# Row maxima of causal attention: narrow products that share a PSUM bank, and another order of the units

## The chip, the cores and the metric

The kernel runs on one core of a Trainium2 chip. The metric is the device time of one execution in microseconds (us). TensorE (PE in the profile, PEld for its weight loads) does the matrix products, VectorE (DVE), ScalarE (ACT) and GpSimd (POOL) work beside it, and SyncE (SP) issues the transfers. PSUM is the memory that TensorE writes: eight banks, each of 512 f32 columns on 128 partitions.

## What is computed

The input x is 4 sequences of 1024 tokens with 128 channels. First comes a causal attention with 16 heads of 8 channels, on a layer norm of x:

```
Q, K, V = heads of (x @ W_dq) @ W_uq, (x @ W_dkv) @ W_uk, (x @ W_dkv) @ W_uv
scores  = Q K^T / sqrt(8), keys after the query masked
out     = softmax(scores) V @ W_o
x       = x + layernorm(out)
```

Then two layers of windowed attention with a gated MLP follow, on a layer norm of x. The change touches only the causal attention, and in it only the maxima of the rows of the scores, which the softmax subtracts before the exponential.

## The kernel before, in words

**Stages and groups.** The causal attention works through 16 stages. A stage is one sequence and four heads (HG = 4). For each stage the scores are computed twice. The first time queries lie on the partitions, so that VectorE can take each query's maximum over the keys. The second time keys lie on the partitions, with the negated maximum added inside the product (12 further rows of the operands), so that ScalarE can take exp at once and TensorE can multiply by V. The second pass of a stage is 12 groups (EXP_GROUPS, L316), n0 to n11 below: n0 to n3 belong to the first 512 queries, with 512, 384, 256 and 128 columns, n4 to n11 to the other 512, with 512 columns in n4 to n8, then 384, 256 and 128. Each group has four score products, one for each head.

**The units of the maxima.** The first pass is cut into units (MAX_UNITS, L315): row tile i (128 queries, 0 to 7), head j, block kc of 512 keys. Row tiles 0 to 3 need one block (128, 256, 384, 512 columns), row tiles 4 to 7 a whole block of 512 and a second one of 128, 256, 384 or 512 columns. That makes 48 units a stage. The last block of a row tile crosses the diagonal: VectorE adds the mask and takes the maximum in one custom instruction, followed by a read of the accumulator (L1491). The whole block before it takes a plain reduction (L1493). The order before is row tile, head, block, so from row tile 4 on a wide whole block and a narrow masked one alternate.

**How the two passes are woven.** Units run ahead of the groups: 32 before the first group, then 8 a group for the first six groups of the kernel, then 4 a group (max_until, L324). So in every stage from the second on, units of the coming stages are spread like this: n0 has row tile 2, n1 row tile 3, n2 and n3 row tile 4, n4 and n5 row tile 5, n6 and n7 row tile 6, n8 and n9 row tile 7, n10 row tile 0, n11 row tile 1. In TensorE's program (L1011) each of a group's four score products is followed by a quarter of the group's units. After the units come, where they are due, the turning of the maxima (turn_maxima, L728) and of the outputs (turn_outputs, L738), and after every odd group the products with V of two earlier groups (values, L712). "The pair n2/n3" below is two groups with their V products. V products that begin a new half of the queries also wait for ScalarE's copy of the finished output (copy_outputs, L1104).

**The ring.** Unit products go to the tensor psM, four banks used in turn (MRING = 4, m_bank). Every unit has a slot of its own (max_slot, L355). The turned outputs of the attention take slots of the same ring (o_slot, L361). TensorE waits with a unit until VectorE has read the slot four before it:

```
ge(pe, m_read, r - MRING + 1)
```

VectorE waits with slot r until `m_ready` is r + 1 and adds one to `m_read` with each unit (maximum, L1482). merge (L1495) joins the two blocks' maxima after the last unit of a stage, outputs (L1500) divides the turned outputs, and GpSimd's cut_maxima (L1329) splits the maxima into three bf16 parts. They are turned, copied by ScalarE and sent by SyncE to the operand (send_maxima, L621), and the second pass of the stage needs them. The scores of the second pass have a ring of three banks (psE), in which narrow groups already share a bank (score, L696).

**Work of other parts in this stretch.** In stages 4 to 6, 8 to 10 and 12 to 14 the output projection and two layer norms of the sequence before are also done, with VectorE's statistics (moments_m, L1522) between the maxima.

Of the kernel before, what the change touches and what calls it, by code (L numbers as in the profile page):

```python
# [21 lines left out]
ALU = mybir.AluOpType  # L22
ACT = mybir.ActivationFunctionType
AX = mybir.AxisListType

B, S, D = 4, 1024, 128
P = 128
NT = B * S // P
TB = S // P
NCH = NT // 4  # L30
NH, DK, DC = 16, 8, 32
HG = 4
# [3 lines left out]
ROWS = NPAIR * DK  # L36
# [5 lines left out]
NEG = -1e30  # L42
# [10 lines left out]
def ge(eng, sem, count):  # L53

    if isinstance(count, int) and count <= 0:
        return
    eng.wait_ge(sem, count)
# [254 lines left out]
            pipelined(pe, NCH, 2, [(2, transposes), (3, heads)])  # L312


MAX_UNITS = [(i, j, kc) for i in range(TB) for j in range(HG) for kc in range(i // 4 + 1)]  # L315
EXP_GROUPS = [(qc, kt) for qc in range(2) for kt in range(4 * qc + 4)]  # L316
NMU, NGR = len(MAX_UNITS), len(EXP_GROUPS)
NM_A = sum(1 for i, _, _ in MAX_UNITS if i < 4)
NSTAGE = B * NG
# [3 lines left out]

def max_until(G):  # L324

    return max(0, min(NSTAGE * NMU, LEAD + min(FAST * (G + 1), SKEW + HG * (G + 1))))


def max_group(u):

    G = -1
    while max_until(G) <= u:
        G += 1
    return G


def o_turn_group(e, qc):

    return e * NGR + (8 if qc == 0 else NGR + 4)
# [12 lines left out]
    return (4, 4, 2, 1)[max(0, kt - 4 * qc)]  # L352


def max_slot(u):  # L355

    G = max_group(u)
    return u + sum(1 for e in range(NSTAGE) for qc in range(2) if o_turn_group(e, qc) < G)


def o_slot(e, qc):  # L361

    G = o_turn_group(e, qc)
    return max_until(G) + sum(1 for e2 in range(NSTAGE) for q2 in range(2) if o_turn_group(e2, q2) < G)


def masks_until(G):
# [36 lines left out]


E_SLOT, E_TOTAL = e_slots()
M_TAIL = NSTAGE * NMU + 2 * NSTAGE - 3
LAST_G = NSTAGE * NGR - 1


def m_bank(r):

    return r % 4 if r < M_TAIL else 2


def in_output_bank(b, h, project):

    return b == B - 1 and (h == 1 or project)
# [70 lines left out]
def attend_and_layers(nc, io, sb):  # L489


    with ExitStack() as ctx:
        def early(name, shape, dt=F32):
            return ctx.enter_context(nc.sbuf_tensor(name, shape, dt))

        def sem(name):
            return ctx.enter_context(nc.semaphore(name))

        arena = sb["arena"]
        NPROB, NRING, MRING = 5, 3, 4  # L500
        qs, ks, v_flat = sb["qs"], sb["ks"], sb["v_flat"]
# [4 lines left out]
        nm = early("a_nm", [P, 2, 2, TB, HG])  # L506
# [59 lines left out]
        with ExitStack() as banks:  # L566
            psM = banks.enter_context(nc.psum_tensor("a_psM", [P, MRING, 512], F32))
# [14 lines left out]
        m_ready, m_read = sem("m_ready"), sem("m_read")  # L582
# [100 lines left out]
        def _(pe):  # L683
            def max_unit(u):

                s, (i, j, kc) = u // NMU, MAX_UNITS[u % NMU]
                g, r = s % NG, max_slot(u)
                if u % NMU == 0:
                    pe.wait_ge(stack_in[g], 32 * (s // NG + 1))
                n = min(512, (i + 1) * P - 512 * kc)  # L690
                out = psM[:, m_bank(r), 0:n]
                ge(pe, m_read, r - MRING + 1)
                pe.matmul(out, qs[0:ROWS, g, j, i * P:(i + 1) * P], ks[0:ROWS, g, j, 512 * kc:512 * kc + n],  # L693
                          start=True, stop=True).then_inc(m_ready, 1)

            def score(G, j):  # L696

# [40 lines left out]
            def turn_outputs(e, qc):  # L738
                r = o_slot(e, qc)
                pe.wait_ge(o_copied, 2 * e + qc + 1)  # L740
                if r < M_TAIL:
                    ge(pe, m_read, r - MRING + 1)
                elif r < M_TAIL + 2:
                    pe.wait_ge(m_read, r)
                    pe.wait_ge(hT_copied, r - M_TAIL + 2)
                out = psM[:, m_bank(r), :] if r < M_TAIL + 2 else psO
                for t in range(4):
                    mm = pe.transpose(out[:, t * P:(t + 1) * P], oT[:, qc, t * P:(t + 1) * P], sb["ident"])
                mm.then_inc(m_ready, 1)
# [14 lines left out]
            def project_o(b, h):  # L764
# [6 lines left out]
                if in_output_bank(b, h, True):  # L771
                    pe.wait_ge(m_read, M_TAIL + 3)
                    out, done = psO, m_o_done
# [234 lines left out]
            for u in range(max_until(-1)):  # L1008
                max_unit(u)
# [468 lines left out]
        def _(dve):  # L1478
# [3 lines left out]
            def maximum(u):  # L1482
                s, (i, j, kc) = u // NMU, MAX_UNITS[u % NMU]
                r = max_slot(u)
                n = min(512, (i + 1) * P - 512 * kc)
                if s > 1 and u % NMU in (0, NM_A):
                    dve.wait_ge(nm_parts, 2 * (s - 2) + (u % NMU == NM_A) + 1)
                dve.wait_ge(m_ready, r + 1)
                scores, low = psM[:, m_bank(r), 0:n], nm[:, s % 2, kc, i, j:j + 1]
                if kc == i // 4:  # L1490
                    dve.tensor_tensor_reduce(scores, scores, sb["mask_q"][:, 512 - n:512], -1.0, -3.0 * NEG, ALU.add, ALU.min, low).then_inc(m_read, 1)  # L1491
                else:
                    dve.tensor_reduce(low, scores, AX.X, ALU.max, negate=True).then_inc(m_read, 1)  # L1493

            def merge(s):  # L1495
                dve.wait_ge(m_read, max_slot(s * NMU + NMU - 1) + 1)
# [485 lines left out]
```

## Time and profile before

| | us |
|---|---|
| three runs: median (lowest, highest) | 1361.78 (1360.88, 1364.80) |
| profiled execution, its own time | 1359.25 |
| profiled execution, span from first to last instruction | 1357.5 |
| causal attention's groups, first to last score product | about 83 to 583 |
| mean granted TensorE clock over the span | 0.97 of full |

The table's first line is what the forecast is compared with. The profile is one execution, and durations come from it. In the profile a line number is that of the kernel before. A matmul's recorded duration holds its way through the array, so two matmuls overlap in the record; the distance between two starts tells what one costs the engine. The rows themselves stand in a section of their own below.

### The profile page before, as it was taken

The page shows a single profiled execution, that of the slowest core. Times are in us where ns is not written, and L with a number is a line of the kernel's source. Part 1 is how long each engine was busy: PE and PEld are TensorE (multiplying, and loading weights), DVE is VectorE, ACT ScalarE, POOL GpSimd, SP SyncE. Part 2 cuts the span into 40 slices and gives each one's busy share as a digit, 9 for nine tenths or more (in the row PEclk, how much of TensorE's full clock was granted, in tenths as well). Part 3 has the DMA queues.
Part 4 walks back from the last instruction along what each step waited for, and adds up shares of the span by engine and source line. Part 5 has one row for each costly group of instructions (what it writes and reads, how often), then busy time and mean ns, then how long its engine had stood idle before and what let it go on. Part 6 is the DMA issues. An engine that isn't in the chain of part 4 may idle for free. (4 is left out here: it accounts for less than half of the span.)

```text
span 1357.5 us, 30203 instructions
## 1 busy us (share of the span) xinstructions
PE 1235.0 (91%) x10501; PEld 702.8 (52%) x10501; DVE 1116.1 (82%) x2928; ACT 926.9 (68%) x2463; POOL 745.5 (55%) x753
## 2 busy tenths in 40 slices
PE   4689999999999999888899999799899999997895
PEld 2323434434433443356666666566466666666663
DVE  5788888988898889679799999766589999997675
ACT  4526776777787777577888888533588888885344
POOL 1112211332231133378999999533699999997244
PEclk9959999999999999899999999899999999999998
DMA  4432111111111101011111111100112111111001
GB/s 109 131 101 75 45 56 46 58 55 52 51 39 42 55 21 35 25 33 36 42 33 33 29 29 33 48 0 1 24 25 54 33 33 33 25 33 25 1 17 47
DMA packets 35486, 56.46 MB, mean 42 GB/s; under 512 B 6898, under 2 KB 22652, under 8 KB 33020
## 3 DMA queue, kind: packets, MB, share of 16 engines
q1 hardware_dynamic: 34760, 54.39, 15.3%
q8 instruction: 85, 1.39, 0.4%
q14 instruction: 65, 0.53, 0.1%
q10 hardware_dynamic: 576, 0.15, 0.1%
HBM read 27.78 MB, written 8.39 MB: 27 GB/s over the span
## 5 line engine op out<-in xcount | busy, mean ns | idle before, releaser
L1095 ACT ACTIVATE a_prob<-a_psE 128x512 f32<-128x512 f32 (+1 forms) x608 | 306.3, 582 | 137.6 <-PE a_psE L707 136.2
L693 PE MATMUL a_psM<-a_ks,a_qs 72*128 72x512 bf16 (+3 forms) x768 | 249.1, 344 | 12.8 <-DVE a_nm L1493 5.2
L1491 DVE CUSTOM_DVE_ANT_0 a_psM<-a_psM,mask_q 128x384 f32<-128x384 f32 (+3 forms) x512 | 242.0, 507 | 13.7 <-PE a_psM L693 13.2
L1327 POOL TENSOR_SCALAR_AFFINE_SELECT a_prob<-a_prob 128x512 f32<-128x512 f32 x128 | 81.3, 638 | 312.3 <-ACT a_prob L1095 311.2
L707 PE MATMUL a_psE<-a_qs,a_ks 84*128 84x512 bf16 (+3 forms) x768 | 240.4, 334 | 11.5 <-ACT a_prob L1095 5.9
L1386 POOL TENSOR_TENSOR w_rn<-w_ssm,mhalf 128x16 f32<-128x16 f32 x64 | 220.3, 3443 | 48.8 <-DVE w_ssm L1581 33.4
L1493 DVE TENSOR_REDUCE a_nm<-a_psM 128x1 f32<-128x512 f32 x256 | 175.4, 685 | 45.3 <-PE a_psM L693 45.3
L1205 ACT ACTIVATE w_prob<-w_psS,w_bias 128x128 f32<-128x128 f32 x512 | 179.9, 377 | 21.0 <-DVE w_bias L1607 20.9
L1371 POOL TENSOR_TENSOR w_t<-w_raw,w_sin 128x256 f32<-128x256 f32 x252 | 176.4, 733 | 0.0
L1376 POOL TENSOR_TENSOR w_rot<-w_t,w_t 128x1024 f32<-128x1024 f32 x63 | 148.5, 2357 | 8.6 <-issue 0.4
L707 PEld LDWEIGHTS a_psE<-a_qs,a_ks 84*128 84x128 bf16 x768 | 74.8, 99 | 149.2 <-ACT a_prob L1095 66.1
L723 PE MATMUL psO<-a_prob,v_all 128*32 128x512 f32 (+3 forms) x1536 | 148.2, 502 | 0.0
L806 PE MATMUL w_psQK<-w_wqkv,w_hT 128*128 128x512 f32 x256 | 120.9, 593 | 1.4 <-DVE w_t L1588 1.4
L693 PEld LDWEIGHTS a_psM<-a_ks,a_qs 72*128 72x128 bf16 x768 | 76.1, 99 | 84.3 <-DVE a_nm L1491 27.2
L1205 ACT ACTIVATION_READ_ACCUMULATOR w_prob<-w_psS,w_bias 128x1 f32 x512 | 111.1, 217 | 0.0
L1607 DVE TENSOR_REDUCE w_bias<-w_psS 128x4 f32<-128x512 f32 x128 | 87.7, 686 | 25.9 <-PE w_psS L851 25.6
L828 PE MATMUL w_psT_<-ident,w_rot 128*128 128x128 f32 x512 | 70.6, 282 | 33.7 <-DVE w_rot L1596 26.8
L828 PEld LDWEIGHTS w_psT_<-ident,w_rot 128*128 128x128 f32 x512 | 56.4, 143 | 79.8 <-DVE w_rot L1596 68.5
L1596 DVE TENSOR_TENSOR w_rot<-w_rot,w_rn 128x1024 f32<-128x1024 f32 x64 | 77.9, 1218 | 23.5 <-POOL w_rot L1376 23.5
L1212 ACT ACTIVATE w_pT<-w_psT_ 128x512 f32<-128x512 f32 x64 | 38.2, 597 | 71.2 <-PE w_psT_ L860 71.2
L860 PE MATMUL w_psT_<-ident,w_prob 128*128 128x128 f32 x512 | 80.6, 281 | 2.9 <-DVE w_prob L1620 2.5
L1620 DVE TENSOR_TENSOR w_prob<-w_prob,w_rden 128x1024 f32<-128x1024 f32 x64 | 78.5, 1227 | 2.2
(189 smaller groups left out, 2386.8 us busy)
## 6 DMA issues: line engine op xcount, KB each, us to landing
a_qs<-q_parts SPq DMA_DIRECT2D x16, 576.0 KB
a_ks<-k_parts SPq DMA_DIRECT2D x16, 576.0 KB
q_parts<-p_parts SPq DMA_DIRECT2D x24, 128.0 KB
k_parts<-p_parts SPq DMA_DIRECT2D x24, 128.0 KB
w_vb__707<-w_v__691 SPq DMA_DIRECT2D x16, 128.0 KB, 2.2
w_vb__708<-w_v__691 SPq DMA_DIRECT2D x16, 128.0 KB, 2.3
w_vb__708<-w_v__692 SPq DMA_DIRECT2D x16, 128.0 KB, 2.2
w_vb__709<-w_v__692 SPq DMA_DIRECT2D x16, 128.0 KB, 2.4
```

The costliest lines, as they stand in the source:

```text
L693: pe.matmul(out, qs[0:ROWS, g, j, i * P:(i + 1) * P], ks[0:ROWS, g, j, 512 * kc:512 * kc + n], start=True, stop=True).then_inc(m_ready, 1)
L707: mm = pe.matmul(psE[:, r % NRING, j % share * w:(j % share + 1) * w], ks[0:KROWS, g, j, kt * P:(kt + 1) * P], qs[0:KROWS, g, j, q0:q0 + w ...
L723: mm = pe.matmul(psO[32 * j:32 * j + 32, q0:512], v_flat[:, col + j * VA:col + j * VA + 32], prob[G % NPROB][:, j, 0:512 - q0], start=(kt ...
L806: pe.matmul(psQK[:, w, :], hT[T % 2][:, 0:P], wqkv[:, first:first + INNER], start=True, stop=True).then_inc(qk_done, 1)
L828: i = pe.transpose(psT[w][:, c * P:(c + 1) * P], rot[:, T % 2, w * INNER + c * P:w * INNER + (c + 1) * P], sb["ident"])
L1095: act.activation(prob[G % NPROB][:, j - share + 1:j + 1, 0:w], psE[:, r % NRING, 0:share * w].rearrange("p (j n) -> p j n", j=share), ACT. ...
L1205: i = act.activation(w_prob[:, p, w, c, :], psS[:, w, c * P:(c + 1) * P], ACT.Exp, bias=bias[:, p, n:n + 1], accum_out=den[:, p, n:n + 1])
L1371: i = pool.tensor_tensor(out[:, w, :, half, :], src[:, w, :, 1 - half, :], tab, ALU.mult)
L1376: pool.tensor_tensor(rot[:, T % 2, :], t1[:, T % 2, :], t2[:, :], ALU.add).then_inc(rot_done, 1)
L1386: pool.tensor_tensor(rn[:, T % 2, 0:n], ssm[:, T % 2, 0:n], sb["mhalf"][:, 0:n], ALU.pow).then_inc(rn_done, 1)
L1491: dve.tensor_tensor_reduce(scores, scores, sb["mask_q"][:, 512 - n:512], -1.0, -3.0 * NEG, ALU.add, ALU.min, low).then_inc(m_read, 1)
L1493: dve.tensor_reduce(low, scores, AX.X, ALU.max, negate=True).then_inc(m_read, 1)
```

## The change

The order of the units becomes row tile, block, head. A function max_width gives a unit's columns, max_share how many consecutive units use one bank: four units of 128 columns, two of 256, one of 384 or 512. m_slots hands out the slots in the order of TensorE's program, units of one bank with one slot together, so a stage takes 38 slots for its units where it took 48. TensorE waits for a free bank only before the first unit of a bank and signals only after the last; VectorE waits before the first and signals after the last.

```diff
-MAX_UNITS = [(i, j, kc) for i in range(TB) for j in range(HG) for kc in range(i // 4 + 1)]
+MAX_UNITS = [(i, j, kc) for i in range(TB) for kc in range(i // 4 + 1) for j in range(HG)]
...
+def max_width(u):
+
+    i, _, kc = MAX_UNITS[u % NMU]
+    return min(512, (i + 1) * P - 512 * kc)
+
+
+def max_share(u):
+
+    return max(1, 512 // max_width(u) if max_width(u) != 384 else 1)
+
+
+def m_slots():
+
+    slots, n = {}, 0
+    for G in range(-1, NSTAGE * NGR + HG):
+        for u in range(max_until(G - 1) if G >= 0 else 0, max_until(G)):
+            slots["u", u] = n
+            if u % max_share(u) == max_share(u) - 1:
+                n += 1
+        for e in range(max(0, G // NGR - 1), min(G // NGR + 1, NSTAGE)):
+            for qc in range(2):
+                if o_turn_group(e, qc) == G:
+                    slots["o", e, qc] = n
+                    n += 1
+    slots["o", NSTAGE - 1, 1] = n
+    return slots, n + 1
...
-M_TAIL = NSTAGE * NMU + 2 * NSTAGE - 3
+M_TAIL = M_TOTAL - 3
...
                 n = min(512, (i + 1) * P - 512 * kc)
-                out = psM[:, m_bank(r), 0:n]
-                ge(pe, m_read, r - MRING + 1)
-                pe.matmul(out, qs[0:ROWS, g, j, i * P:(i + 1) * P], ks[0:ROWS, g, j, 512 * kc:512 * kc + n],
-                          start=True, stop=True).then_inc(m_ready, 1)
+                share = max_share(u)
+                at = u % share * n
+                if u % share == 0:
+                    ge(pe, m_read, r - MRING + 1)
+                mm = pe.matmul(psM[:, m_bank(r), at:at + n], qs[0:ROWS, g, j, i * P:(i + 1) * P], ks[0:ROWS, g, j, 512 * kc:512 * kc + n],
+                               start=True, stop=True)
+                if u % share == share - 1:
+                    mm.then_inc(m_ready, 1)
...
-                dve.wait_ge(m_ready, r + 1)
-                scores, low = psM[:, m_bank(r), 0:n], nm[:, s % 2, kc, i, j:j + 1]
+                share = max_share(u)
+                at = u % share * n
+                if u % share == 0:
+                    dve.wait_ge(m_ready, r + 1)
+                scores, low = psM[:, m_bank(r), at:at + n], nm[:, s % 2, kc, i, j:j + 1]
                 if kc == i // 4:
-                    dve.tensor_tensor_reduce(scores, scores, sb["mask_q"][:, 512 - n:512], -1.0, -3.0 * NEG, ALU.add, ALU.min, low).then_inc(m_read, 1)
+                    d = dve.tensor_tensor_reduce(scores, scores, sb["mask_q"][:, 512 - n:512], -1.0, -3.0 * NEG, ALU.add, ALU.min, low)
                 else:
-                    dve.tensor_reduce(low, scores, AX.X, ALU.max, negate=True).then_inc(m_read, 1)
+                    d = dve.tensor_reduce(low, scores, AX.X, ALU.max, negate=True)
+                if u % share == share - 1:
+                    d.then_inc(m_read, 1)
```

max_slot and o_slot now look the slot up in that table. No instruction on data is added or taken away on any engine.

## Rows read from the trace of the kernel before

**Rows 1.** The page's head: busy time, share of the span, instructions of each engine.

```profile
PE 1235.0 (91%) x10501; PEld 702.8 (52%) x10501; DVE 1116.1 (82%) x2928; ACT 926.9 (68%) x2463; POOL 745.5 (55%) x753
```

**Rows 2.** Busy time by stretch: length, PE, PEld, DVE, ACT, POOL, clock, DMA share, GB/s.

```profile
103.29:111.39 8.10, 7.74 (x45) 3.11 (x45) 7.15 (x24) 5.15 (x9) 0.00 (x0) 0.86 0.59 151
...
156.10:185.00 28.90, 28.13 (x212) 11.36 (x208) 25.15 (x85) 20.60 (x42) 6.71 (x16) 1.00 0.18 52
...
246.26:275.61 29.35, 28.48 (x213) 11.54 (x209) 27.56 (x102) 23.39 (x50) 10.72 (x19) 1.00 0.19 58
275.61:305.07 29.46, 28.41 (x213) 11.20 (x209) 26.25 (x93) 23.40 (x50) 8.54 (x18) 1.00 0.20 58
```

**Rows 3.** Waits in stage 2 (156.1 to 185): total us, times, longest.

```profile
DVE a_nm L1493 <- PE a_psM L693: 2.6, 3, 1.5
...
DVE a_psM L1491 <- PE a_psM L693: 1.0, 1, 1.0
```

**Rows 4.** Waits of stages 1 to 14 (127.09 to 543.6), TensorE for VectorE.

```profile
PEld a_psM L693 <- DVE a_nm L1491: 14.4, 51, 0.5
...
PEld a_psM L693 <- DVE a_nm L1493: 12.2, 31, 0.5
...
PEld a_psM L693 <- DVE o_tok L1509: 4.5, 14, 0.3
```

**Rows 5.** Timeline of PE, pair n2/n3 of stage 2: start us, duration us, instruction.

```profile
160.80 0.28 PE L707 MATMUL a_psE<-a_qs,a_ks 84*128 84x256 bf16 x1
160.91 0.38 PE L693 MATMUL a_psM<-a_ks,a_qs 72*128 72x512 bf16 x1
161.13 0.27 PE L707 MATMUL a_psE<-a_qs,a_ks 84*128 84x256 bf16 x1
...
162.15 0.39 PE L693 MATMUL a_psM<-a_ks,a_qs 72*128 72x512 bf16 x1
...
162.96 0.39 PE L693 MATMUL a_psM<-a_ks,a_qs 72*128 72x512 bf16 x1 [0.24 <-DVE a_nm L1493]
...
163.24 0.22 PE L693 MATMUL a_psM<-a_ks,a_qs 72*128 72x128 bf16 x1
163.39 1.71 PE L723 MATMUL psO<-a_prob,v_all 128*32 128x512 f32 x16
```

**Rows 6.** Timeline of DVE, the same pair.

```profile
161.40 0.69 DVE L1493 TENSOR_REDUCE a_nm<-a_psM 128x1 f32<-128x512 f32 x1
162.01 0.29 DVE L1491 CUSTOM_DVE_ANT_0 a_psM<-a_psM,mask_q 128x128 f32<-128x128 f32 x1
...
162.22 0.69 DVE L1493 TENSOR_REDUCE a_nm<-a_psM 128x1 f32<-128x512 f32 x1
...
165.68 0.69 DVE L1493 TENSOR_REDUCE a_nm<-a_psM 128x1 f32<-128x512 f32 x1 [0.90 <-PE a_psM L693]
```

**Rows 7.** Timeline of ACT, the same pair: the copy of the finished output.

```profile
162.00 0.59 ACT L1108 ACTIVATE a_oT<-psO 128x512 f32<-128x512 f32 x1
```

**Rows 8.** Timeline of PE, pair n10/n11 of stage 2.

```profile
182.13 0.22 PE L693 MATMUL a_psM<-a_ks,a_qs 72*128 72x128 bf16 x1
182.19 0.22 PE L707 MATMUL a_psE<-a_qs,a_ks 84*128 84x128 bf16 x1
...
183.15 0.28 PE L693 MATMUL a_psM<-a_ks,a_qs 72*128 72x256 bf16 x1
183.36 1.71 PE L723 MATMUL psO<-a_prob,v_all 128*32 128x512 f32 x16
```

**Rows 9.** Timeline of DVE, the same pair.

```profile
181.99 0.30 DVE L1491 CUSTOM_DVE_ANT_0 a_psM<-a_psM,mask_q 128x128 f32<-128x128 f32 x1
...
182.20 0.33 DVE L1491 CUSTOM_DVE_ANT_0 a_psM<-a_psM,mask_q 128x128 f32<-128x128 f32 x1
...
182.45 0.33 DVE L1491 CUSTOM_DVE_ANT_0 a_psM<-a_psM,mask_q 128x128 f32<-128x128 f32 x1
```

**Rows 10.** Timeline of PE at the kernel's first group.

```profile
83.43 0.61 PE L707 MATMUL a_psE<-a_qs,a_ks 84*128 84x512 bf16 x1 [4.09 <-DMA a_qs<-a_nmT]
```

More of the change, by code:

```diff
@@ L352, in exp_slots @@
     return (4, 4, 2, 1)[max(0, kt - 4 * qc)]
+def max_width(u):
[17 more added lines that the diff above has]
+    return slots, n + 1
+M_SLOT, M_TOTAL = m_slots()
 def max_slot(u):
-    G = max_group(u)
-    return u + sum(1 for e in range(NSTAGE) for qc in range(2) if o_turn_group(e, qc) < G)
+    return M_SLOT["u", u]
 def o_slot(e, qc):
-    G = o_turn_group(e, qc)
-    return max_until(G) + sum(1 for e2 in range(NSTAGE) for q2 in range(2) if o_turn_group(e2, q2) < G)
+    return M_SLOT["o", e, qc]
 def masks_until(G):
```

## The prediction

> **What bounds the kernel now.** I read the page's head first [rows 1]: TensorE is busy for 91% of the span and VectorE for 82%, too close together to name a bound. The change lies in the causal attention alone, so I cut that into its stages. A plain stage takes 28.90 us, with VectorE busy for 25.15 and ScalarE for 20.60 [rows 2]. TensorE shows 28.13, but its records overlap. No engine is full in such a stage: the period comes from engines that wait for each other by turns. VectorE waits 2.6 + 1.0 us a stage for unit products [rows 3], mostly once a pair, while TensorE does the products with V and has at most four units handed over. TensorE in turn waits for VectorE to free a bank [rows 4]: 14.4 + 12.2 + 4.5 = 31.1 us over stages 1 to 14, or 2.2 a stage. Those rows are of the weight loads and overcount, since the product in front is often still running. So the question is what each of these waits holds up, and that shows only in the order of time, pair by pair.
>
> In **pair n2/n3** (row tile 4) [rows 5], cost goes by columns: from 160.80 to 160.91 a score product of 256 columns takes 0.11, from 160.91 to 161.13 a unit of 512 takes 0.22. So 128 columns cost about 0.06. The unit at 162.15 waits for the reduction that started at 161.40 and ended 0.69 later, at 162.09 [rows 6]; the one at 162.96 waits again, for the reduction of 162.22 to 162.91. By columns the whole pair would have been issued 0.7 us sooner than it was. In **pair n10/n11** (row tiles 0 and 1) the units of 128 columns run freely up to 182.13, but the last of 256 columns is issued at 183.15 [rows 8]. A score product of 128 and a unit of 256 cost 0.17 together; they come 0.25 apart instead, because each unit waits for a 128-column read and VectorE does those every 0.25 us [rows 9]. In n8/n9 one unit waits 0.3 for outputs() (14 times in 14 stages, the third row of [rows 4]); in n4/n5 and n6/n7 of a plain stage no unit waits.
>
> **The change, part by part.** All counts of instructions stay, on every engine and queue. What changes is the order, and where the waits stand.
>
> *Pair n2/n3.* Now four units of 512 columns come first, into four banks, and then four of 128 into one bank. By columns: 160.80 + 4 x 0.33 = 162.12 for the start of n3's first score product, 162.18 for its first narrow unit. That unit needs the bank of the first wide one, whose read ends at 162.09 as before, so it hardly waits. The other three don't wait at all. Four times 0.11 leads to a last unit at about 162.5 and, 0.15 later as in [rows 5], the V products at 162.65. They also wait for ScalarE's copy of the output, 162.00 + 0.59 = 162.59 [rows 7]; that is just in time and is what is late next. V products start at 163.39 now. **Gain 0.74.**
>
> *Pair n10/n11.* Four units of 128 columns share a bank, and the 256s use two. The last 256 is issued at 182.19 + 0.06 + 3 x 0.17 = 182.76 instead of 183.15. **Gain 0.39.**
>
> *Pair n8/n9.* Here the order of widths (512 all along) doesn't matter. The last unit still waits for outputs(), which VectorE does behind four reads of the same length. Gain 0.
>
> *Pairs n4/n5 and n6/n7.* No unit waits in a plain stage, so there is nothing to gain. The fifth bank is asked for behind four score products and four units of 512, 8 x 0.22 = 1.8 us after the pair's start. The first read begins some 0.6 after it (165.68, where the V products end at 163.39 + 1.71 = 165.10 [rows 5, 6]) and ends 0.69 later, at 1.3: no new wait. Cost 0, hidden in that slack of 0.5.
>
> *What VectorE pays.* A masked read behind another masked read shows 0.33 and takes 0.25 from start to start, behind a reduction it shows 0.29 and takes 0.21 [rows 6, 9]. In the new order 12 masked reads a stage have moved behind one of their own kind: 12 x 0.04 = 0.5 us more. Four reductions in a row do not occur in the trace before. I take 0.60 from start to start, as from 161.40 to 162.01, where a masked read follows; the bounds are 0.56 and the full 0.69. Second cost: VectorE can begin on the shared bank only when all four units are there. In n10 that is 182.13 + 0.22 + 0.04 = 182.39 instead of 181.99 [rows 8, 9], 0.40 later. In a plain stage both hide: VectorE idles 3.6 us of the stage now [rows 3], 0.90 of it right behind n3 [rows 6]; 25.15 + 0.5 is still well under 28.90 - 1.13 = 27.8. At 165.68 it would have been free for a second; in the new stage it gets its next unit 0.74 earlier and is free 0.1 before it.
>
> *Stages that are short of VectorE.* In stages 5, 9 and 13 VectorE is busy for 27.56 of 29.35 us, in 6, 10 and 14 for 26.25 of 29.46 [rows 2], one of three standing for each kind. There it doesn't idle from n10 to the end of n3, so the first reduction of n2 comes 0.40 later than now (the shared bank of n10), and only what lies behind it is shorter: now the V products start 1.99 behind the reduction's start (163.39 - 161.40), then 0.69 + 0.06 + 3 x 0.11 + 0.15 = 1.23, so 0.76 are won and 0.40 lost. **Gain 0.36** for both pairs together. In three of them n6/n7 has VectorE's statistics at its start, and the fifth unit then waits about 0.1 longer.
>
> *The start.* The first group waits for the first maxima by DMA [rows 10], and these for the 32 units of the lead, a stretch in which VectorE never idles. The last units of the lead come two to a bank, and TensorE gets past them sooner by up to one read of 0.60; I take half, 0.3. In the six groups with 8 units each, the maxima of n3 go through the same chain at the same point, so nothing is won up to 103.29. In the pair after it (8.10 us, clock 0.86 [rows 2]) TensorE waits for VectorE with almost every unit; the V products can start behind four wide reads and a shared one instead of behind the whole alternation, 0.6 sooner, and what stays of the low clock is shorter too. I take 1.0, between 0.3 and 1.7.
>
> **The sum.** Eight boundaries into plain stages (1 to 4, 7, 8, 11, 12): 8 x 1.13 = 9.0. Six into the stages short of VectorE: 6 x 0.36 = 2.2. The start: 0.3 + 1.0. Off go 3 x 0.1. In all 12.2 us. The last stage has no units, and what follows the attention is unchanged. The profiled execution took 1359.25 (span 1357.5), 2.5 below the median of the runs; I take the gain off the median: 1361.8 - 12.2 = 1349.6.
>
> **Rivals.** *A, my forecast:* 1349.6; its own sizes allow 1345 to 1354.
>
> *B, another wait takes the place.* The V products of n3 wait for ScalarE's copy of the output, which has only 0.06 us in hand above. If the copy or the exponentials in front of it come later in most stages, the 0.74 is gone and only n10/n11 pays: 14 x 0.39 = 5.5, 1356.3. For it: ScalarE does have extra work in the stages short of VectorE. Against it: nothing of ScalarE's moves in this pair, since its exponentials hang on the first two score products.
>
> *C, reductions in a row cost their full 0.69.* The rows show a masked read start 0.60 behind a reduction [rows 6], which speaks against it, but no reduction behind a reduction. Three times 0.08 then delay outputs() in n8/n9, where the last unit waits for it: 14 x 0.25 = 3.5 less gain, 1353.1. The Trainium skill, page VectorE: DVE Perf Modes, section The DRAIN you can't avoid, says that the next op does not start until the pipe of the one before is empty. The row at 162.01 contradicts that for the instruction pair it shows.
>
> *D, slower: VectorE is the bound all the way.* If TensorE's lead doesn't shorten the period, the shared banks' late hand-over in n10 (0.40) and the 12 dearer masked reads (0.5) come on top of every one of 14 stages: +12.6, 1374.4. It decides from the point at which VectorE has no idle time to lose; the stages 5, 9 and 13 are nearest to it with 1.8 us left, a plain stage has 3.6. The Trainium skill, page Perfetto Trace Analysis, section Matmuls, speaks for it: independent products should rotate through different banks, so that emptying one overlaps the next product. Filling one bank with four products gives up just that overlap.
>
> *E, every wait for a bank goes:* all 31 us of [rows 4], 1330.7. Against it: the weight loads' waits overcount, and n8/n9 waits for outputs() as before.
>
> **How the numbers follow.** Chances: A 0.57, B 0.15, C 0.11, D 0.08, E 0.04, and 0.05 that gains and costs cancel within 0.3%, which is 4 us and about what a measurement of this kernel can tell from no change. The range takes in A, C and B with a margin: 1341 to 1358. D, E and a part of the rest, under 0.2, are left out. Faster by over 0.3% (below 1357.7) are A, C, E and most of B: 0.84. Within 0.3%: 0.08. Slower: 0.08.
>
> **What would show it right or wrong.** Right: a plain stage of 27.8 us; V products 1.85 us behind the start of pair n2/n3 instead of 2.59; VectorE's idle time ahead of n4 gone; its busy time 25.6 a stage; reductions 0.60 apart. Wrong: the wait ahead of V products on the copy of the output (B); reductions 0.69 apart (C); stages longer than 28.90 with VectorE idle under 1 us (D); plain stages near 26.7 (E).

## The result and the profile after

| | before | after |
|---|---|---|
| median of 7 runs each, us | 1363.21 (1360.70 to 1368.48) | 1355.94 (1353.87 to 1359.77) |
| profiled execution, us (span, mean clock) | 1359.25 (1357.5, 0.970) | 1356.7 (1355.0, 0.969) |

The ratio is 0.995, with a 95% interval of 0.9932 to 0.9968. The change makes the kernel 7.3 us faster, with an interval of 4.4 to 9.3 by that ratio. The forecast was 12.2, outside the interval. Medians and ratios here and below leave out the one execution on record that was slow throughout, 1445.67 us at a mean granted clock of 0.83.

The head of the page of the changed kernel answers to [rows 1]:

```profile
PE 1233.4 (91%) x10501; PEld 708.1 (52%) x10501; DVE 1121.9 (83%) x2928; ACT 925.5 (68%) x2463; POOL 745.5 (55%) x753
```

VectorE has 5.8 us more to do, in the same 2928 instructions. No share has moved by more than a point, so again only the stages tell anything. Windows of the changed kernel (columns as in [rows 2]) for stages 2, 4, 5, 6 and 14:

```profile
158.04:186.08 28.04, 27.63 (x213) 11.62 (x209) 25.62 (x88) 20.43 (x42) 6.64 (x16) 1.00 0.20 55
214.54:245.91 31.37, 30.63 (x232) 13.93 (x229) 26.58 (x99) 22.21 (x45) 6.69 (x16) 1.00 0.14 42
245.91:274.88 28.97, 28.16 (x212) 11.75 (x208) 27.57 (x103) 23.35 (x50) 10.96 (x20) 1.00 0.20 59
274.88:304.31 29.43, 28.48 (x213) 11.56 (x209) 27.11 (x96) 23.42 (x50) 8.48 (x18) 1.00 0.20 58
511.48:541.93 30.45, 29.50 (x205) 11.26 (x202) 26.15 (x89) 23.54 (x50) 8.06 (x18) 0.94 0.13 39
```

And the same view of the kernel before for stage 4, which [rows 2] lacks:

```profile
214.70:246.26 31.56, 30.76 (x232) 13.72 (x229) 26.59 (x100) 22.48 (x45) 6.98 (x18) 1.00 0.15 42
```

A plain stage went from 28.90 to 28.04, stage 4 only from 31.56 to 31.37, stage 5 from 29.35 to 28.97, stage 6 from 29.46 to 29.43, and stage 14 grew, at a clock of 0.94. Cut at the score products into pairs, before/after in us:

| stages | n0/1 | n2/3 | n4/5 | n6/7 | n8/9 | n10/11 | won in all |
|---|---|---|---|---|---|---|---|
| 1, 2, 3, 7, 11 (2 shown) | 4.69/4.70 | 4.24/3.58 | 4.65/4.87 | 5.93/5.93 | 5.88/5.85 | 3.51/3.11 | 4.59 |
| 4, 8, 12 (4 shown) | 5.71/5.72 | 4.24/3.58 | 4.75/5.64 | 6.58/6.58 | 6.77/6.75 | 3.51/3.10 | 0.70 |
| 5, 9, 13 (5 shown) | 4.69/4.90 | 4.69/4.22 | 4.66/4.97 | 5.93/5.93 | 5.88/5.85 | 3.51/3.10 | 1.18 |
| 6, 10 (6 shown) | 4.69/4.90 | 4.80/4.78 | 4.66/4.87 | 5.93/5.93 | 5.88/5.85 | 3.51/3.10 | 0.07 |
| 14 | 4.69/4.90 | 4.80/6.28 | 4.66/4.97 | 5.93/5.93 | 5.88/5.85 | 2.52/2.52 | -1.97 |

(Stages 3, 7 and 11 differ from the stage shown in n10/n11: 4.30, 3.95 and 3.95 before, 3.54, 3.54 and 3.79 after.) Together stages 1 to 14 won 4.57 us. Pair n2/n3 of stage 14 alone lost 1.5 against its twins in stages 6 and 10; without that it would be 6.1. Stage 0 won 0.72. Outside these stages the two profiled executions differ by this: the first score product comes 3.64 later (87.07 for 83.43), stage 15 is 1.20 shorter up to its last score product, what follows that is 0.31 longer. That gives 3.64 - 0.72 - 4.57 - 1.20 + 0.31 = -2.5 us, the difference of the spans. So one pair of traces understates the gain, and what is compared below is stages, not spans.

The waits of stages 1 to 14 that answer to [rows 4]:

```profile
PEld a_psM L724 <- DVE a_nm L1527: 12.8, 30, 0.5
PEld a_psM L724 <- DVE a_nm L1529: 8.4, 24, 0.4
PEld a_psM L724 <- DVE o_tok L1547: 5.3, 14, 0.4
```

From 31.1 us they went to 26.5, in 68 waits instead of 96: fewer waits, but longer ones (0.39 in the mean, 0.32 before). VectorE's waits in stage 2, as in [rows 3]:

```profile
DVE a_nm L1529 <- PE a_psM L724: 1.7, 2, 1.4
DVE a_psM L1527 <- PE a_psM L724: 0.4, 1, 0.4
```

Now the order of time, as in [rows 5]: TensorE in pair n2/n3 and the start of n4/n5, stage 2 (start us, duration us, instruction).

```profile
162.74 0.28 PE L740 MATMUL a_psE<-a_qs,a_ks 84*128 84x256 bf16 x1
...
164.07 0.22 PE L740 MATMUL a_psE<-a_qs,a_ks 84*128 84x128 bf16 x1
164.13 0.22 PE L724 MATMUL a_psM<-a_ks,a_qs 72*128 72x128 bf16 x1
...
164.48 0.22 PE L724 MATMUL a_psM<-a_ks,a_qs 72*128 72x128 bf16 x1
164.68 1.71 PE L756 MATMUL psO<-a_prob,v_all 128*32 128x512 f32 x16
166.32 0.39 PE L740 MATMUL a_psE<-a_qs,a_ks 84*128 84x512 bf16 x1
...
168.08 0.60 PE L781 MATMUL a_psM<-ident,a_oT 128*128 128x128 f32 x4
168.52 0.38 PE L740 MATMUL a_psE<-a_qs,a_ks 84*128 84x512 bf16 x1
```

VectorE at the same time, and ScalarE's copy, as in [rows 6, 7]:

```profile
163.35 2.48 DVE L1529 TENSOR_REDUCE a_nm<-a_psM 128x1 f32<-128x512 f32 x4
165.75 0.29 DVE L1527 CUSTOM_DVE_ANT_0 a_psM<-a_psM,mask_q 128x128 f32<-128x128 f32 x1
...
165.96 0.33 DVE L1527 CUSTOM_DVE_ANT_0 a_psM<-a_psM,mask_q 128x128 f32<-128x128 f32 x1
...
166.21 0.33 DVE L1527 CUSTOM_DVE_ANT_0 a_psM<-a_psM,mask_q 128x128 f32<-128x128 f32 x1
```

```profile
163.94 0.59 ACT L1141 ACTIVATE a_oT<-psO 128x512 f32<-128x512 f32 x1
```

No unit waits any more in this pair. The V products start 164.68 - 162.74 = 1.94 behind the pair's start (before: 2.59), 0.20 behind the last unit and 0.15 behind the end of the copy. Four reductions in a row take 2.48 = 3 x 0.60 + 0.68. In n4 there is something else: n5's first score product comes at 168.52, 2.20 behind the pair's start. Before it was 1.98 (167.02 for a pair that started at 165.04), and ScalarE's eight exponentials of the pair, which took 4.04 us in all, now take 4.25. First before, then after:

```profile
167.02 0.38 PE L707 MATMUL a_psE<-a_qs,a_ks 84*128 84x512 bf16 x1
165.52 4.04 ACT L1095 ACTIVATE a_prob<-a_psE 128x512 f32<-128x512 f32 x8 [1.40 <-PE a_psE L707]
```

```profile
166.81 4.25 ACT L1128 ACTIVATE a_prob<-a_psE 128x512 f32<-128x512 f32 x8 [1.29 <-PE a_psE L740]
```

Pair n10/n11 of stage 2, TensorE and VectorE, as in [rows 8, 9]:

```profile
182.97 0.28 PE L740 MATMUL a_psE<-a_qs,a_ks 84*128 84x256 bf16 x1
183.09 0.22 PE L724 MATMUL a_psM<-a_ks,a_qs 72*128 72x128 bf16 x1
...
184.23 0.27 PE L724 MATMUL a_psM<-a_ks,a_qs 72*128 72x256 bf16 x1
184.43 1.71 PE L756 MATMUL psO<-a_prob,v_all 128*32 128x512 f32 x16
```

```profile
183.97 0.30 DVE L1527 CUSTOM_DVE_ANT_0 a_psM<-a_psM,mask_q 128x128 f32<-128x128 f32 x1 [0.41 <-PE a_psM L724]
...
184.19 0.33 DVE L1527 CUSTOM_DVE_ANT_0 a_psM<-a_psM,mask_q 128x128 f32<-128x128 f32 x1
```

The units of 256 columns come 0.17 apart and nothing waits; VectorE begins only when the fourth narrow unit is there, having been idle for 0.41. Its first read starts 1.00 behind the pair's start, where it was 0.49 before (181.99 and 181.50).

Pair n4/n5 of stage 4, TensorE and VectorE, is where the 0.66 of n2/n3 went (this pair took 4.75 before and takes 5.64 now):

```profile
226.24 0.63 PE L781 MATMUL a_psM<-ident,a_oT 128*128 128x128 f32 x4 [0.24 <-DVE a_nm L1529]
```

```profile
223.47 0.66 DVE L1562 BATCH_NORM_STATS2 m_stats<-m_attn 128x6 f32<-128x128 f32 x3
...
225.41 2.48 DVE L1529 TENSOR_REDUCE a_nm<-a_psM 128x1 f32<-128x512 f32 x4
227.80 0.25 DVE L1544 RECIPROCAL a_rec<-a_psM 128x16 f32<-128x16 f32 x1
```

VectorE takes the statistics of the sequence before (moments_a, sent out at n2) behind n2's reductions. It starts on n4's reductions at 225.41, when TensorE has been in the pair since 223.85. TensorE waits for it with the turned output, starts that at 2.39 behind the pair's start (168.08 - 166.32 = 1.76 in stage 2), and the pair takes 5.64.

Last, stage 14: two windows that share its pair n2/n3, the V products in the second, and the first part of the same pair in stage 6.

```profile
516.38:519.50 3.12, 2.58 (x20) 0.95 (x16) 3.12 (x11) 2.62 (x6) 0.70 (x2) 1.00 0.02 4
519.50:522.66 3.16, 3.16 (x19) 0.60 (x17) 2.25 (x11) 2.13 (x5) 1.62 (x6) 0.50 0.00 0
```

```profile
519.51 3.21 PE L756 MATMUL psO<-a_prob,v_all 128*32 128x512 f32 x16
```

```profile
279.78:282.91 3.13, 2.59 (x20) 0.95 (x16) 3.13 (x11) 2.63 (x6) 0.71 (x2) 1.00 0.52 138
```

In stage 14 TensorE was busy for 2.58 of 3.12 us, with waits for VectorE, which was busy all the time. Then the granted clock fell from 1.00 to 0.50 (1.2 GHz), and 16 products that take 1.71 took 3.21. Stage 6 shows the same busy times and no fall behind them.

### The profile page after: what moved, and what is told of

Read it like the earlier page. It is cut to its first block and busy times, and to the rows that moved or that the text cites. A ratio compares the mean times of both kernels' runs of the same rounds, so it can differ in the third digit from the quotient of the medians.

```text
span 1355.0 us, 30203 instructions
## 1 busy us (share of the span) xinstructions
PE 1233.4 (91%) x10501; PEld 708.1 (52%) x10501; DVE 1121.9 (83%) x2928; ACT 925.5 (68%) x2463; POOL 745.5 (55%) x753
## 3 DMA queue, kind: packets, MB, share of 16 engines
q8 instruction: 85, 1.39, 0.4%
## 5 line engine op out<-in xcount | busy, mean ns | idle before, releaser
L724 PE MATMUL a_psM<-a_ks,a_qs 72*128 72x512 bf16 (+3 forms) x768 | 241.9, 343 | 8.6 <-PEq L106 3.2
L1527 DVE CUSTOM_DVE_ANT_0 a_psM<-a_psM,mask_q 128x384 f32<-128x384 f32 (+3 forms) x512 | 234.3, 523 | 13.2 <-PE a_psM L724 9.0
L1529 DVE TENSOR_REDUCE a_nm<-a_psM 128x1 f32<-128x512 f32 x256 | 158.9, 683 | 34.8 <-PE a_psM L724 33.8
```

Source lines behind the costliest of these rows:

```text
L724: mm = pe.matmul(psM[:, m_bank(r), at:at + n], qs[0:ROWS, g, j, i * P:(i + 1) * P], ks[0:ROWS, g, j, 512 * kc:512 * kc + n], start=True, s ...
L1527: d = dve.tensor_tensor_reduce(scores, scores, sb["mask_q"][:, 512 - n:512], -1.0, -3.0 * NEG, ALU.add, ALU.min, low)
L1529: d = dve.tensor_reduce(low, scores, AX.X, ALU.max, negate=True)
```

## The experiments

The two parts of the change were taken apart first, then the order changed inside, then the load moved. Diffs are against the changed kernel unless another is named. The first eight were executed once each; they stand beside the kernel before at 1366.98 us (first four) and 1361.96 us (next four), each one execution too. Two single times a few microseconds apart say nothing; what these eight show is read from their stages.

**The order alone.** Every unit keeps a bank of its own.

```diff
 def max_share(u):
-    return max(1, 512 // max_width(u) if max_width(u) != 384 else 1)
+    return 1
```

> The block order alone, with a bank for each unit as before. My theory: the order by itself costs. In n4/n5 of a plain stage four wide units stand ahead of n5's first score product, so the pair takes 4.87 us as in the changed kernel and not 4.65. In n2/n3 each of the four narrow units waits for one of the four wide reads, the last of them for the fourth, so the pair gets longer than before, about 4.9 where before had 4.24 and the changed kernel 3.58. n10/n11 is back at 3.50. Stage 2 about 29.8 us against 28.90 before. Rival: the 0.22 in n4/n5 come from the shared banks (the ring hands out its banks in another rhythm); then n4/n5 is 4.65 here.

1388.52 us. Stage 2 takes 29.84: pairs 4.69, 4.95, 4.87, 5.93, 5.85, 3.55. In the waits of stages 1 to 14 TensorE's for reductions, 12.2 us before, are now

```profile
PEld a_psM L724 <- DVE a_nm L1529: 33.3, 81, 0.5
```

Four reductions in a row free their banks 0.60 apart, and n3's narrow units need these banks one by one: n2/n3 is 0.71 longer than before, where the shared bank makes it 0.66 shorter. Pair n4/n5 has its 4.87 here as well, so the shared banks have no part in that; the order has. And five of the fourteen n2/n3 pairs took 6.3 to 6.9 us, with the clock down. Stages 1 to 14 are 20.7 us longer than before: 14 x 0.71 + 14 x 0.22 = 13.0, and most of the rest in those five pairs and the pairs behind them. A window over the one of stage 1:

```profile
138.50:144.90 6.40, 5.49 (x35) 1.85 (x34) 4.05 (x15) 2.17 (x4) 2.44 (x7) 0.76 0.03 5
```

**The shared bank alone**, in the order from before. In it only row tiles 0 and 1 have narrow units in a row, so only theirs share.

```diff
-MAX_UNITS = [(i, j, kc) for i in range(TB) for kc in range(i // 4 + 1) for j in range(HG)]
+MAX_UNITS = [(i, j, kc) for i in range(TB) for j in range(HG) for kc in range(i // 4 + 1)]
...
 def max_share(u):
+    if MAX_UNITS[u % NMU][0] > 3:
+        return 1
```

> The old order, and banks shared only in row tiles 0 and 1 (in the old order no others have narrow units in a row). My theory: n10/n11 takes 3.10 us, all other pairs of a plain stage are as before (4.69, 4.24, 4.65, 5.93, 5.88), so stage 2 takes 28.5. In stages 5 and 6, where VectorE is short, the shared bank is handed over 0.40 late and that eats the gain: they stay within 0.1 of 29.36 and 29.47. Rival: the late hand-over is harmless, and stages 5 and 6 gain the 0.40 too (28.96, 29.07).

1367.19 us, no gain that one execution could show. Stage 2 is down to 28.50, all of it in n10/n11 (3.10), as expected. But in the stages short of VectorE the late hand-over costs more than it was expected to: n0/n1 takes 4.90 and n2/n3 is longer too (stage 5: 4.96 for 4.69, so the stage takes 29.52 for 29.35, where within 0.1 of it was expected), and in stages 6, 9, 10, 13 and 14 n2/n3 took 6.0 to 7.1 us. The window of stage 6 over that pair, as in stage 14 above:

```profile
277.60:284.80 7.20, 6.09 (x37) 1.73 (x34) 5.28 (x20) 4.78 (x11) 2.39 (x7) 0.76 0.21 58
```

With these five pairs stages 1 to 14 take 423.62 us, 7.1 more than before. So the order alone only costs, and the shared bank alone wins its 0.40 in n10/n11 and loses more elsewhere. In n2/n3 the two are worth something only together: the order puts the narrow units side by side, the shared bank lets them pass.

**Row tile 5 with its narrow block first**, to test the theory that n4/n5's 0.22 are the columns ahead of n5's first score product.

```diff
-MAX_UNITS = [(i, j, kc) for i in range(TB) for kc in range(i // 4 + 1) for j in range(HG)]
+MAX_UNITS = [(i, j, kc) for i in range(TB) for kc in ((1, 0) if i == 5 else range(i // 4 + 1)) for j in range(HG)]
```

> The changed kernel, but row tile 5 takes its narrow block (256 columns) in n4 and its whole block in n5. My theory (columns ahead of n5's first score product let ScalarE run dry): n4/n5 of a plain stage goes from 4.87 to 4.65 us or a little under. Rival (the shared banks or the ring's rhythm cost the 0.22): it stays at 4.87, since two shared banks are still in the pair. Stages 4, 8 and 12 keep most of their longer n4/n5 (5.5 to 5.6 against 4.75 before) if that comes from the bank behind VectorE's statistics.

1357.48 us, stages 1 to 14 408.18 in sum (411.92 in the changed kernel, 1.5 of it for the fall of the clock in stage 14). n4/n5 is 4.73 in a plain stage, with 4.65 expected; the four wide units that now stand in n5 cost stage 5 something in n6/n7 (6.39 for 5.93). In stage 4, where the longer n4/n5 was expected to stay, it takes 5.02 for 5.64. The turned output there is issued 1.47 behind the pair's start (226.97), unwaited:

```profile
228.44 0.60 PE L781 MATMUL a_psM<-ident,a_oT 128*128 128x128 f32 x4
```

By the table of slots this order makes it wait for the last of n2's wide reads, which comes before VectorE's statistics; in the changed kernel it waits for the first wide read of n4, which comes behind them.

**The order for row tile 4 alone**, so that row tiles 5 to 7 go head by head as before.

```diff
-MAX_UNITS = [(i, j, kc) for i in range(TB) for kc in range(i // 4 + 1) for j in range(HG)]
+MAX_UNITS = [(i, j, kc) for i in range(5) for kc in range(i // 4 + 1) for j in range(HG)]
+MAX_UNITS += [(i, j, kc) for i in range(5, TB) for j in range(HG) for kc in range(2)]
...
 def max_share(u):
+    if MAX_UNITS[u % NMU][0] > 4:
+        return 1
```

> Block order in row tile 4 alone; row tiles 5 to 7 alternate wide and narrow as before, and share no bank; row tiles 0, 1 and the narrow block of 4 share. My theory: a plain stage has 3.58 in n2/n3, 4.65 in n4/n5 and 3.10 in n10/n11, 27.8 us in all, 0.2 less than the changed kernel. Rival (shared banks cause the 0.22): n4/n5 is 4.65 here too, so this run alone does not tell them apart, but with the order-only kernel it does. Whole kernel about 3 us under the changed one, apart from the spread between executions.

1357.38 us. Stage 2:

```profile
155.63:183.48 27.85, 27.45 (x213) 11.57 (x209) 25.27 (x88) 20.41 (x42) 6.65 (x16) 1.00 0.20 55
```

n4/n5 is back at 4.65, n2/n3 stays at 3.58, and VectorE has 0.35 less to do than with the order everywhere. But n4/n5 of stages 4, 8 and 12 still takes 5.53, 5.53 and 5.64 (5.64, 5.53 and 5.63 in the changed kernel): the four wide units in a row aren't what makes it long there. Two n2/n3 pairs (stages 10 and 14) took 6.1, so the sum of stages 1 to 14 is 411.25, and the 3 us expected for the whole kernel don't show.

**The statistics moved.** If VectorE is the bound of n2 to n5 in stage 4 and of n0 to n3 in stage 6, its statistics must go elsewhere: moments_a(b, 0) from n2 to n7, moments_x(b, 1) from n11 of stage 5 to its n7.

```diff
-                        if project_group(b, h) + 1 == G:
+                        if project_group(b, h) + 6 - 5 * h == G:
                             moments_a(b, h)
-                        if project_group(b, 1) + 8 + 6 * h == G:
+                        if project_group(b, 1) + 8 + 2 * h == G:
                             moments_x(b, h)
```

> The changed kernel, with two of the four statistics of the sequence before moved on VectorE to the end of n7, where VectorE idles: moments_a(b, 0) from n2 to n7 of stages 4, 8 and 12, moments_x(b, 1) from n11 to n7 of stages 5, 9 and 13. My theory: in those stretches VectorE's work is the bound, so what TensorE gains in n2/n3 is given back. Then n4/n5 of stages 4, 8 and 12 falls from 5.5 to 5.6 us to the plain 4.87, and n0/n1 and n2/n3 of stages 6, 10 and 14 fall from 4.90 and 4.78 to 4.7 and 3.6 to 4.2, so about 0.7 in three stages and 0.8 in three, 4.5 us in all. Rival (these stages are longer through TensorE's and ScalarE's own extra work there): the pairs stay as they are, and the 1.2 us of moved statistics show up as a longer n8/n9.

1348.74 us. n4/n5 of stage 4, whole and the turned output in it:

```profile
220.34:225.31 4.97, 4.89 (x44) 2.60 (x41) 4.81 (x18) 4.36 (x9) 0.96 (x3) 1.00 0.00 0
```

```profile
222.09 0.60 PE L781 MATMUL a_psM<-ident,a_oT 128*128 128x128 f32 x4
```

It comes 1.75 behind the pair's start, unwaited, and the pair is 0.67 shorter. Stage 6 is 28.52 for 29.43, with n0/n1 at 4.70 and n2/n3 at 4.05. In stage 5 n8/n9 pays, 6.1 for 5.85. Stages 1 to 14 take 406.21 in sum, 5.7 less than in the changed kernel, of which 1.5 is the fall of the clock in stage 14; 4.5 were expected.

**Two to a bank** in place of four.

```diff
 def max_share(u):
-    return max(1, 512 // max_width(u) if max_width(u) != 384 else 1)
+    return 2 if max_width(u) <= 256 else 1
```

> The changed kernel, with only two units of 128 columns to a bank instead of four. VectorE can start in n10 about 0.3 us sooner. My theory (in the stages short of VectorE the late hand-over costs): n0/n1 of stages 5, 6, 9, 10 goes from 4.90 back to 4.7 and n2/n3 of stage 6 gets shorter by 0.1 to 0.3; in plain stages n10/n11 stays at 3.10, while n2/n3 gets longer by 0.2 to 0.3, because the second bank of n3's narrow units waits for the second wide read. Rival (the hand-over is harmless): n0/n1 of stages 5 and 6 stays at 4.90 and only the loss in n2/n3 shows.

1355.48 us. Stage 2 is 28.32, with n2/n3 at 3.87 (3.58 with four, 4.24 with one); n0/n1 of stages 5 and 6 is back at 4.69 (4.90 with four). But n2/n3 gives that back, where it was expected to get shorter in stage 6: 4.44 for 4.22 in stage 5, 4.99 for 4.78 in stage 6. Over n0 to n3 both kernels take 9.1 us in stage 5 and 9.68 in stage 6, with VectorE busy all through. So two to a bank only shifts the loss in these stages, and in n2/n3 of a plain stage it is 0.29 worse than four.

**Row tile 4 alone and the statistics moved:**

> Block order in row tile 4 alone, and the two statistics moved to n7. If both theories hold, a plain stage takes 27.85 us, stages 4, 8 and 12 about 30.5 (31.3 without the move), stages 5 and 9 28.7, stages 6 and 10 28.0 to 28.6. TensorE then waits less for VectorE in n2/n3, so no stage after 0 should show TensorE's clock at half. The kernel would be some 7 to 9 us faster than the changed one.

1348.84 us, stages 1 to 14 403.61 in sum, 2.6 under the run with the statistics moved alone, and no long n2/n3 pair. What follows stage 15's last score product took 2.4 us longer here, so the two totals are equal.

**The kernel before with the statistics moved:**

> The kernel before, with the two statistics moved to n7. It tells how much of the gain is the move's own. My theory: the old order never uses the room in stages 4, 8 and 12 (n4/n5 there took 4.75, near the plain 4.65), so little is won in them, at most 0.1 each; in stages 6, 10 and 14 the pair n2/n3 falls from 4.80 to 4.24, so 0.6 in three stages, 2 us in all. Rival: the move alone brings the whole 4.5 us that it brings on the changed kernel.

1359.85 us, stages 1 to 14 417.11, with one long pair (n2/n3 of stage 5, 6.15 for 4.68). Two microseconds under the run beside it can't be told from none by one execution.

**The same kernels, timed.** The last four were timed together with the kernel before (median 1362.7 of 17 runs). First the change with the statistics moved:

> The changed kernel with the statistics of the sequence before moved away from the short pairs (moments_a(b,0) from n2 to n7 in stages 4, 8, 12; moments_x(b,1) from n11 to n7 in stages 5, 9, 13), timed beside the kernel before. Theory (these stages gave the gain back because VectorE was their bound): in the single looks the sum of stages 1 to 14 fell from 411.9 to 406.2 us, of which some 2 us was one fall of the clock; expected 3 to 5 us under the changed kernel, so 1350.5 to 1353, ratio to before 0.991 to 0.993. Rival (the single look was only free of falls of the clock, the statistics hide anyway): 1354 to 1356, ratio 0.995.

1349.53 us, ratio 0.9903 (0.988 to 0.9926). The rival's 0.995 is outside; the gain is a little more than the 0.991 to 0.993 expected. Then with the order for row tile 4 alone:

> The same with the new order and the shared bank for row tile 4 alone (row tiles 5 to 7 head by head, as before the change). Theory (the order costs 0.22 us wherever wide units of row tile 5 stand before the first score product of n5): 14 times 0.2 less than with the order everywhere, so 2.5 us under the run with the statistics moved alone: 1348 to 1350.5, ratio to before 0.989 to 0.991. Rival (what the order wins in row tiles 5 to 7 is worth as much): no difference between the two within 0.5 us.

1347.09 us, ratio 0.9889 (0.9864 to 0.9915). The medians are 2.4 apart as expected, though the intervals overlap; by stages the sum is 403.56 against 406.37. Then with moments_x(b, 1) at n9 of stage 5:

```diff
-                        if project_group(b, 1) + 8 + 2 * h == G:
+                        if project_group(b, 1) + 8 + 4 * h == G:
```

> As the one before it, but moments_x(b,1) at n9 of stages 5, 9, 13 in place of n7. At n7 it made n8/n9 longer, 6.21 against 5.88 us, VectorE idle only 0.08 us there. Theory (VectorE falls behind over n7 to n9): at n9 the pair n8/n9 is back at 5.88, n10/n11 has 0.58 us of idle VectorE against 1.2 us of statistics and grows by 0 to 0.6 us, so 0 to 1 us (3 times 0.33) under the run with n7. Rival (the statistics have to be paid once wherever they stand): equal within 0.3 us, with n10/n11 at 3.4 or more.

1347.82 us, ratio 0.9887 (0.9864 to 0.9911), no different from the run before it by medians. Its stages 2, 4, 5 and 6:

```profile
154.80:182.65 27.85, 27.45 (x212) 11.55 (x209) 25.27 (x86) 20.40 (x42) 6.66 (x16) 1.00 0.19 55
210.93:241.34 30.41, 29.98 (x232) 13.94 (x229) 26.35 (x98) 22.18 (x45) 6.66 (x16) 1.00 0.16 43
241.34:270.14 28.80, 28.17 (x212) 11.69 (x209) 27.75 (x110) 23.33 (x50) 11.13 (x21) 1.00 0.21 59
270.14:298.48 28.34, 27.81 (x212) 11.40 (x209) 25.78 (x89) 23.14 (x50) 8.32 (x17) 1.00 0.22 61
```

n8/n9 is back at 5.88 and n10/n11 stays at 3.11, so stage 5 takes 28.80 for 29.00: the statistics hide in n10/n11's idle time. The sum of stages 1 to 14, 402.82, is the lowest of all, 0.7 under the run before it. Last, the kernel before with the statistics moved:

> The kernel before the change with the same move of the statistics (n2 to n7, n11 to n7). Theory (there VectorE is not the bound of n4/n5, so the move gains little without the change): by the stages of the single look 0.56 us won in stages 6, 10, 14 each, 0.1 in 4, 8, 12, and 0.32 lost in 5, 9, 13, so 1.0 us less than before: ratio 0.999, 0.997 to 1.0. Rival (the move is worth the same with or without the change): 3 to 5 us less, ratio 0.9965 or lower.

1361.11 us, the median of eleven executions, ratio 0.9996 (0.9976 to 1.0015). The move alone gives nothing that can be measured. Its stages 4 and 6:

```profile
213.86:245.33 31.47, 30.67 (x232) 13.74 (x229) 26.71 (x100) 22.39 (x45) 6.97 (x18) 1.00 0.15 42
...
275.00:303.91 28.91, 28.14 (x213) 11.36 (x209) 25.15 (x86) 23.39 (x50) 8.29 (x17) 1.00 0.20 60
```

The change alone gives 7.3 us (in the runs of the result), the move alone 0.5 by its ratio, between 3.3 won and 2.0 lost, both together 13.2, and with the order for row tile 4 alone about 15: the versions that beat both kernels. The move pays only once TensorE is ahead: it lets the stages with statistics keep what n2/n3 has won.

## Why the prediction was right, and where its sum was off

The direction, the place and the mechanism held: the wait for banks in n2/n3 and n10/n11 went, and the time is in the range. The sum was 12.2, of which 7.3 came. That the time is in the range owes something to its width, which was set to take in rival B: 1355.94 lies 6.3 from the forecast and 0.4 from B's 1356.3, and only the trace tells that B's mechanism is not what made it so. Step by step:

*Pair n2/n3, 0.74.* 0.66 by the trace. The first narrow unit came at 1.39 behind the pair's start (forecast 1.38), the last at 1.74 (1.70). The V products followed 0.20 later, not 0.15.

*Pair n10/n11, 0.39.* 0.40.

*Pair n8/n9, 0.* 0.03 won. The wait for outputs() is still there, 14 times.

*Pairs n4/n5 and n6/n7, cost 0, "hidden in that slack of 0.5".* This step failed for n4/n5: 0.22 lost in nearly every stage. I had looked for a wait for a bank. There is none; what counts is what stands in TensorE's queue in front of n5's first score product. Head by head that was two wide and two units of 256 columns, by blocks it is four wide ones, two times 0.11 more. ScalarE gets n5's scores later by that, and its eight exponentials of the pair take 4.25 us for 4.04. The run with the order alone showed it without any shared bank, and the runs with the narrow block first (4.73) and with row tile 4 alone (4.65) took it away again. n6/n7 has cost nothing but 0.06 in stage 13, so its "3 x 0.1" didn't come either.

*Eight plain boundaries, 8 x 1.13.* Three of the eight, stages 4, 8 and 12, were not plain, and that is the second failed step. I took their n2/n3 for a plain one, and it did win its 0.66. But the statistics sent out at n2 take VectorE 1.2 us, and when TensorE is 0.66 earlier, VectorE is what n4/n5 waits for: 0.78 to 0.89 lost there. The columns don't come on top of that: with row tile 4 alone the loss stays. The slack that I read in [rows 3] is that of stage 2. Moving the statistics took n4/n5 of stage 4 from 5.64 to 4.97, which shows the cause; the 0.22 left over the 4.75 of before are the columns.

*VectorE's reads and reductions.* 25.62 us of work in a plain stage (25.6 forecast), reductions 0.60 apart. Rival C is out. The late hand-over was 0.51 (1.00 behind the pair's start for 0.49) and not 0.40; it hides in a plain stage, as forecast.

*Stages short of VectorE, 0.36 each.* Counted from n10 of the stage before to n3, stages 5, 9 and 13 won 0.40 - 0.21 + 0.47 = 0.66, stages 6 and 10 won 0.40 - 0.21 + 0.02 = 0.21. The mean, 0.44, is near the forecast, but the two kinds are not alike: in 6 and 10 the late hand-over stands (0.21 in n0/n1) and n2/n3 wins nothing, since the statistics at n11 of the stage before leave VectorE behind right through n3. With those statistics moved, n0/n1 of stage 6 is 4.70 and n2/n3 4.05. What keeps it above the plain 3.58 was not tested; another small task of VectorE (shift_m) stands at n0 there.

*The start, 1.3.* From the first unit to the first score product 17.92 became 17.86: 0.06 of the 0.3. Stage 0 took 42.95 for 43.66: 1.47 won in n4/n5, but 1.05 lost in n10/n11, which takes 3.10 to 4.9 in the executions seen, with the clock. That this gain is the change's is not shown: the kernel before with the statistics moved, whose stage 0 is the same as before, took 42.84 in both its profiled executions.

*The rivals.* B: the V products start 0.15 behind the end of the copy, so it was near, but the gain of n2/n3 is there. D, the bound at VectorE, is half true: not in the plain stages, but in the stages with statistics. The rule named there (the Trainium skill, Perfetto Trace Analysis, section Matmuls) fits 0.21 us of n0/n1, where two to a bank do better than four, but n2/n3 gives these back, and for the sum it doesn't hold here, since a ring of four banks holds more units ahead when narrow ones share. E didn't come: the waits add up to 26.5 us still.

**The account.** Stages 1 to 14 were to win 10.9: by pairs, n10/n11 14 x 0.39 = 5.5, n2/n3 and n0/n1 8 x 0.74 - 6 x 0.03 = 5.7, n4/n5 nothing, 0.3 off for n6/n7. Summed over the 14 stages (stage 14's n2/n3 taken as its twins'), n10/n11 won 5.3, n2/n3 6.8 less 1.3 in n0/n1, so 5.5, and n8/n9 0.4; n4/n5 lost 5.1. So what fell short is one pair: 2.5 in eleven stages for the columns and 2.6 in stages 4, 8 and 12 for the late VectorE. The start adds between nothing and 0.7, where 1.3 was forecast. That gives 6.1 to 6.8 us, where the medians say 7.3 (4.4 to 9.3 by the interval).

Still open: why the clock falls in one n2/n3 pair and not in its twin. The runs show only where it does.

## What to carry to other kernels

A shorter wait on one engine is a gain only as far as the next one follows: price it with the neighbour's load in that very stage, and not with a typical one. When instructions change places, count what comes to stand in front of each instruction that feeds another engine, even when no wait is added. And where a change makes the place of a side task matter, move the side task: here that brought some 6 us on top of the change, and nothing that could be measured without it.

## What the runs showed of the hardware

Four reductions of 512 columns in a row start 0.60 us apart, though each shows 0.68. The Trainium skill, VectorE: DVE Perf Modes, section The DRAIN you can't avoid, says that the next op does not start before the pipe of the one before is empty, and adds that one which is not held starts earlier. These rows show the second: 0.08 us earlier than the record of the first ends.

The granted clock fell in pairs in which TensorE was far from idle but had waited several times for VectorE: behind 2.58 busy of 3.12 us it went to 0.50 (1.2 GHz). Against the same pair of a twin stage that kept its clock, where there is one, a fall costs 1.0 to 1.5 us (1.50 in the changed kernel, 6.28 for 4.78). In the profiled executions n2/n3 was hit in five stages with the order alone, five with the shared bank alone, two with row tile 4 alone, one each in the changed kernel, with two to a bank and in the first profiled execution of the kernel before with the statistics moved, none in the rest. The two kernels that were hit most are those in which VectorE holds TensorE back longest in this pair: in the pairs hit there the V products start 3.3 to 4.2 us behind the pair's start, in those hit elsewhere 3.0 to 3.4. The Trainium skill, TensorE: Matmul & The Clock Gate, Part 1, says that the gate goes by how busy TensorE has been of late. That the falls came behind waits fits it, but stage 6, with the same busy times and no fall, shows that these rows alone don't tell when it falls. So a wait of 0.4 us, repeated in one pair, can cost more than it shows.

The first stretch of the kernel, which the change doesn't touch, varied by 3.6 us between two traces. The same window of before, then of after:

```profile
40.00:50.00 10.00, 4.88 (x23) 3.19 (x24) 8.31 (x30) 6.98 (x21) 2.41 (x4) 1.00 0.56 140
```

```profile
40.00:50.00 10.00, 7.90 (x27) 4.52 (x26) 6.01 (x19) 5.29 (x13) 1.21 (x2) 0.75 0.42 108
```

Part of the difference goes with the granted clock, which was 0.75 in this window for 1.00. But 1.2 us of it was there earlier, at a clock of 1.00 in both: SyncE's first issue of q_parts came at 26.48 for 25.32. What made that part is open. Either way the whole attention shifts. With kernels a few microseconds apart, two profiled executions must be compared from a common instruction on.
